# A GRU with a mixture of experts on one core: input product ahead of the steps, preparation in another order

## What is computed

```python
gi = x @ W_ih + b_ih            # 512 -> 3 * 512
gh = h @ W_hh + b_hh
r = sigmoid(i_r + h_r); z = sigmoid(i_z + h_z)
n = tanh(i_n + r * h_n)
h = (1 - z) * n + z * h
```

## Time and profile before

| | us |
|---|---|
| median of 3 runs | 913.2 (912.21 to 913.89) |
| the profiled execution | 913.26 |
| its span in the trace | 911.5 |
| TensorE matmul busy | 810.2 (89%) |
| VectorE busy | 634.6 (70%) |
| ScalarE (ACT) busy | 414.3 (45%) |
| GpSimd (POOL) busy | 178.2 (20%) |

### The profile page before, as it was taken

One profiled execution on the slowest core, in us unless ns is written; L12 is line 12 of the kernel. 1 busy time (PEld: TensorE's weight loads), 2 busy tenths in 40 slices (PEclk: granted clock), 3 DMA queues, 4 the chain that ended last, 5 costly groups with the idle time before them and its releaser, 6 DMA issues.

```text
span 911.5 us, 28124 instructions
## 1 busy us (share of the span) xinstructions
PE 810.2 (89%) x11698; PEld 533.4 (59%) x11699; DVE 634.6 (70%) x2087; ACT 414.3 (45%) x852; POOL 178.2 (20%) x454
## 2 busy tenths in 40 slices
PE   5979899997999999999957145999999999999996
PEld 2436565576999899999947143444444444444442
DVE  6868989765888888888875666766775766774500
ACT  0747566543454454545434302834283347416600
POOL 1002212122333333433320001012102100110011
PEclk9989999998999999999987557999999999999999
DMA  9800000000000000000013561247143715360011
GB/s 343 304 0 2 2 1 3 2 3 3 4 5 4 4 4 5 4 4 4 4 29 160 147 223 47 97 136 208 24 138 94 212 16 186 69 193 12 1 24 23
DMA packets 20165, 62.57 MB, mean 69 GB/s; under 512 B 2064, under 2 KB 2064, under 8 KB 17424
## 3 DMA queue, kind: packets, MB, share of 16 engines
q1 hardware_dynamic: 15744, 52.46, 16.6%
q0 software_dynamic: 3584, 8.42, 5.2%
q10 hardware_dynamic: 720, 0.03, 0.1%
HBM read 52.49 MB, written 12.62 MB: 71 GB/s over the span
## 4 chain that ended last, share of the span: by engine, by line
PE 69%; DVE 20%; issue 4%; ACT 3%; DMA 1%; POOL 0%; DVEq 0%; ACTq 0%; POOLq 0%
PE ps L376 18%; PE ps L538 18%; PE ps L551 18%; PE ps L368 8%; DVE wa L1047 4%; DVE wa L1052 3%; DVE halves L1063 3%; ACT wa L648 2%; PE ps L480 2%; PE ps L386 2%; DVE ocand L1056 1%; PE ps L518 1%; PE ps L526 1%; DMA bg_sb<-in_bg 1%; DVE big L965 1%
## 5 line engine op out<-in xcount | busy, mean ns | idle before, releaser
L376 PE MATMUL ps<-halves,wa 128*128 128x64 f16 x8448 | 290.6, 194 | 7.9 <-DVE halves L1063 1.6
L376 PEld LDWEIGHTS ps<-halves,wa 128*128 128x128 f16 x8448 | 274.2, 98 | 35.4 <-DVE halves L1063 15.9
L538 PE MATMUL ps<-wb,big 128*128 128x512 f16 x768 | 166.9, 379 | 1.5 <-DVE wb L1351 1.5
L551 PE MATMUL ps<-big 128*128 128x512 f16 x768 | 166.9, 379 | 0.0
L648 ACT ACTIVATE wa<-ps,un_gates 128x128 f32<-128x128 f32 x288 | 100.1, 365 | 139.0 <-PE ps L376 132.5
L1047 DVE SCALAR_TENSOR_TENSOR wa<-ps,bhn_s,wa 128x64 f32<-128x64 f32 x288 | 80.2, 278 | 72.2 <-ACT wa L648 72.2
L538 PEld LDWEIGHTS ps<-wb,big 128*128 128x128 f16 x768 | 74.7, 98 | 91.5 <-issue 1.7
L551 PEld LDWEIGHTS ps<-big 128*128 128x128 f16 x768 | 75.2, 98 | 89.9
L653 ACT ACTIVATE wa<-wa,un_gates 128x64 f32<-128x64 f32 x288 | 99.1, 344 | 57.5 <-DVE wa L1052 51.1
L368 PE MATMUL ps<-hx,wb 128*128 128x512 f16 x432 | 109.7, 386 | 4.9 <-DVEq L1022 4.9
L713 ACT ACTIVATE hx<-ps,un_hid_in 128x512 f32<-128x512 f32 x64 | 43.7, 683 | 112.4 <-PE ps L538 112.4
(11 more groups left out here) (178 smaller groups left out, 686.2 us busy)
## 6 DMA issues: line engine op xcount, KB each, us to landing
wa<-in_w SPq DMA_DIRECT2D x32, 1024.0 KB, 5.9
hs_rows<-big SPq DMA_DIRECT2D x8, 516.0 KB, 6.2
big<-in_w_ih SPq DMA_DIRECT2D x3, 1024.0 KB, 11.4
hx<-in_x_t SPq DMA_DIRECT2D x3, 1024.0 KB, 20.2
big<-in_w_hh SPq DMA_DIRECT2D x4, 768.0 KB, 16.5
wa<-in_x_t SPq DMA_DIRECT2D x1, 1024.0 KB, 5.2
hx<-hs_rows,idx POOLq DMA_INDIRECT x16, 3.7
out<-hx,idx_out POOLq DMA_INDIRECT x16, 4.8
```

The source lines that it names most:

```text
L376: mm = pe.matmul(gate_ps[:, j, g, :], whh_parts[:, k, w, (4 * g + j) * P:(4 * g + j + 1) * P], halves[:, src, k, h, :], start=False, stop= ...
L538: mm = pe.matmul(ps[:, m % 2, :], w1p[:, w, k, m * P:(m + 1) * P], tokT[:, t, k, :], start=(k == 0 and n == 0), stop=(k == KD - 1 and n == 2))
L551: mm = pe.matmul(ps[:, 2 + g % 2, :], hid[:, h, k, g * P:(g + 1) * P], w2p[:, w, k, :], start=(k == 0 and n == 0), stop=(k == KH - 1 and n ...
```

## The change

The first loads become eight pieces of 256 KB (128 x 512 float32), x_first and W_ih's first third by k. TensorE's first four tiles go k by k, each when its pieces are there. The 12 tiles of the first chunk use all eight banks (`gi_bank`), and the rough steps wait for all twelve to be kept. `PREFILL` = 24 fills (two tiles) run ahead of the wait for the diagonal; `filled(i)` says how many are done when step i begins, up to 432, so that step 22 has 12 left and step 23 none. `kept_by` and `split_by` follow from it. On VectorE the bias sum comes behind the first maxima, the maxima of W_hh run in a row, and W_ih's low halves, x's and most of the first chunk's r/z low halves move behind gates_known; the maximum of the last two x chunks comes ahead of most of them. POOL fills turn in place of VectorE. ACT rounds W_ih and x ahead of its fourth tile.

```diff
+        PREFILL = 24
+        def filled(i):
+            return min(PREFILL + FILL_STEP * i, 3 * GI_MMS)
+        def gi_bank(t):
+            return t % 8 if t < 12 else 4 + t % 4
+        def kept_by(i):
+            return 12 + (PREFILL if i < 0 else min(filled(i) + FILLS[0], 3 * GI_MMS)) // (3 * KD)
         def split_by(i):
-            return 12 + 3 * (i + (i % STEPS_C == STEPS_C - 1)) // 2
+            return kept_by(i - 1) if i >= 0 else 12
...
-            sp.dma_start(x_first, x_t[:, CHUNK_ORDER[0], :, :]).then_inc(S["x_loaded"][0], 16)
-            for g in range(3):
+            for k in range(KD):
+                sp.dma_start(x_first[:, k, :], x_t[:, CHUNK_ORDER[0], k, :]).then_inc(S["first_loaded"][k], 16)
+                sp.dma_start(wih_sb[:, k, 0:D], wih_src[:, k, 0:D]).then_inc(S["first_loaded"][k], 16)
+            for g in range(1, 3):
...
-                if t >= 4:
-                    pe.wait_ge(S["gi_kept"], t - 3)
+                if t >= 8:
+                    pe.wait_ge(S["gi_kept"], t - 7 if t < 16 else t - 3)
-            pe.wait_ge(S["x_loaded"][0], 16)
-            for m in range(12):
+            for k in range(KD):
+                pe.wait_ge(S["first_loaded"][k], 32)
+                for m in range(4):
+                    mm = pe.matmul(ps[:, gi_bank(m), :], wih_sb[:, k, m * P:(m + 1) * P], x_first[:, k, :],
+                                   start=(k == 0), stop=(k == KD - 1))
...
+            for m in range(4, 12):
...
             def gates_rough(src, i):
-                n = FILL_STEP * i
+                n = filled(i)
...
+            fill(0, PREFILL)
             pe.wait_ge(S["diag_ready"], 1)
             pe.wait_ge(S["whh_high"], KD)
+            pe.wait_ge(S["gi_kept"], 12)
...
-                    fill(FILL_STEP * i, FILL_STEP * i + FILL_STEP)
+                    fill(filled(i), filled(i + 1))
...
-            for m in range(4):
+            for m in range(3):
                 first_tile(m)
-            wih_high(0)
-            wih_high(1)
-            first_tile(4)
-            wih_high(2)
-            first_tile(5)
-            wih_high(3)
+            for k in range(KD):
+                wih_high(k)
+            act.wait_ge(S["x_loaded"][1], 16)
             for k in range(KD):
                 x_high(0, k)
-            first_tile(6)
+            first_tile(3)
+            first_tile(4)
             act.wait_ge(S["gates_known"], 1)
             whh_high(0)
+            first_tile(5)
+            whh_high(1)
+            first_tile(6)
+            whh_high(2)
             first_tile(7)
-            whh_high(1)
-            whh_high(2)
-            first_tile(8)
             whh_high(3)
-            for m in range(9, 12):
+            for m in range(8, 12):
                 first_tile(m)
...
+            for t in range(12, kept_by(-1)):
+                tile(t)
...
-                for t in range(12 + 3 * i // 2, 12 + 3 * (i + 1) // 2):
+                for t in range(kept_by(i - 1), kept_by(i)):
...
             pool.tensor_tensor(warm[:, :], ones[:, 0:1], ones[:, 0:1], ALU.mult).then_inc(S["warmed"], 1)
+            for k in range(KD):
+                pool.tensor_tensor(turn[:, k, 0:P], ident[:, :], ident[:, :], ALU.mult).then_inc(S["turn_ready"], 1)
...
-            dve.wait_ge(S["x_loaded"][0], 16)
+            for k in range(KD):
+                dve.wait_ge(S["first_loaded"][k], 32)
...
-            for k in range(KD):
-                dve.tensor_copy(turn[:, k, 0:P], ident[:, :])
...
-            for m in range(4):
-                rz_low(m)
...
-                if k < KD - 1:
-                    wih_low(k)
-                if k in (1, 2):
-                    rz_low(3 + k)
...
-            wih_low(KD - 1)
-            rz_low(6)
+            rz_low(0)
...
             dve.sem_inc(S["gates_known"], 1)
-            for k in range(KD):
-                x_low((0, k))
-            rz_low(7)
+            wih_low(0)
+            rz_low(1)
             for n in range(2, NC_):
                 dve.wait_ge(S["x_loaded"][n], 16)
             link(dve.tensor_reduce(peak[:, X1:X1 + 1], hx[:, 2 * KD * GCOLS:KD * N], AX.X, ALU.max,
                                    apply_absolute_value=True))
             dve.sem_inc(S["peak_ready"], 1)
+            wih_low(1)
+            rz_low(2)
+            wih_low(2)
+            rz_low(3)
+            wih_low(3)
+            for k in range(KD):
+                x_low((0, k))
+                if k % 2:
+                    rz_low(4 + k // 2)
...
             dve.sem_inc(S["gi_known"], 1)
+            rz_low(6)
+            rz_low(7)
```

More of the change, by code:

```diff
@@ L211, in gru_moe @@
         S["wih_loaded"] = [sem(f"wih_loaded_{g}") for g in range(3)]
+        S["first_loaded"] = [sem(f"first_loaded_{k}") for k in range(KD)]
         S["whh_loaded"] = [sem(f"whh_loaded_{k}") for k in range(KD)]
@@ L244, in gru_moe @@
         GI_MMS = 12 * KD * 3
-        assert FILL_STEP * STEPS_C == GI_MMS
+        PREFILL = 24
+        assert FILL_STEP * STEPS_C == GI_MMS and PREFILL % (3 * KD) == 0
+        def filled(i):
+            return min(PREFILL + FILL_STEP * i, 3 * GI_MMS)
         CHUNK_ORDER = (3, 0, 1, 2)
@@ L258, in gru_moe @@
             (c, 4 * g + j) for c in CHUNK_ORDER[1:] for j in range(KD) for g in range(3))
+        def gi_bank(t):
+            return t % 8 if t < 12 else 4 + t % 4
         def rz_count(t):
             return sum(m < 8 for _, m in TILES[:t])
+        def kept_by(i):
+            return 12 + (PREFILL if i < 0 else min(filled(i) + FILLS[0], 3 * GI_MMS)) // (3 * KD)
         def split_by(i):
-            return 12 + 3 * (i + (i % STEPS_C == STEPS_C - 1)) // 2
+            return kept_by(i - 1) if i >= 0 else 12
+        assert split_by(STEPS_C - 1) >= 24 and split_by(2 * STEPS_C - 1) >= 36 and split_by(FILLED - 1) == 48
+        assert kept_by(2 * STEPS_C - 1) <= 38
         def x_scale(q):
@@ L339, in bank_free @@
             def bank_free(t):
-                if t >= 4:
-                    pe.wait_ge(S["gi_kept"], t - 3)
-            pe.wait_ge(S["x_loaded"][0], 16)
-            for m in range(12):
+                if t >= 8:
[5 more added lines that the diff above has]
+                                   start=(k == 0), stop=(k == KD - 1))
+                    if k == KD - 1:
+                        mm.then_inc(S["gi_mm"], 1)
+            for m in range(4, 12):
                 bank_free(m)
@@ L350, in _ @@
                 for k in range(KD):
-                    mm = pe.matmul(ps[:, 4 + m % 4, :], wih_sb[:, k, m * P:(m + 1) * P], x_first[:, k, :],
+                    mm = pe.matmul(ps[:, gi_bank(m), :], wih_sb[:, k, m * P:(m + 1) * P], x_first[:, k, :],
                                    start=(k == 0), stop=(k == KD - 1))
@@ L367, in fill @@
                         bank_free(tile)
-                    mm = pe.matmul(ps[:, 4 + tile % 4, :], wih_parts[:, w, k, m * P:(m + 1) * P],
+                    mm = pe.matmul(ps[:, gi_bank(tile), :], wih_parts[:, w, k, m * P:(m + 1) * P],
                                    x_parts[:, q, t, k, :], start=(left == 0), stop=(left == KD * 3 - 1))
@@ L471, in _ @@
             pe.wait_ge(S["gru_over"], 1)
-            pe.wait_ge(S["turn_ready"], 1)
+            pe.wait_ge(S["turn_ready"], KD + 1)
             for n in range(NT):
@@ L600, in keep_tile @@
                         act.wait_ge(S["gi_low"], rz_count(t) - GI_RING + 1)
-                    act.activation(gi_full[:, rz_count(t) % GI_RING, :], ps[:, 4 + t % 4, :], ACT.Identity,
+                    act.activation(gi_full[:, rz_count(t) % GI_RING, :], ps[:, gi_bank(t), :], ACT.Identity,
                                    bias=bias_gi[:, q, m:m + 1], scale=sc).then_inc(S["gi_kept"], 1)
                 else:
-                    act.activation(gi[:, c, m % 4, 2, :], ps[:, 4 + t % 4, :], ACT.Identity, bias=bsum_g[:, m:m + 1],
+                    act.activation(gi[:, c, m % 4, 2, :], ps[:, gi_bank(t), :], ACT.Identity, bias=bsum_g[:, m:m + 1],
                                    scale=g_sc).then_inc(S["gi_kept"], 1)
@@ L891, in _ @@
             dve.wait_ge(S["steps_made"], 1)
[L892 to L896, removed]
             link_n = [0]
@@ L921, in _ @@
             for g in range(3):
-                dve.wait_ge(S["wih_loaded"][g], 16)
+                if g > 0:
+                    dve.wait_ge(S["wih_loaded"][g], 16)
                 dve.tensor_reduce(chunk_peak[:, g:g + 1], wih_sb[:, :, g * D:(g + 1) * D], AX.XY, ALU.max,
@@ L925, in _ @@
             link_n[0] += 4
-            dve.wait_ge(S["consts_pool"], 1)
-            for k in range(KD):
-                dve.tensor_copy(turn[:, k, 0:P], ident[:, :])
+            dve.wait_ge(S["small_loaded"], 16 * 5)
+            dve.tensor_tensor(bsum[:, 0:8], bih[:, 0:8], bhh[:, 0:8], ALU.add)
+            dve.tensor_copy(bsum[:, 8:12], bih[:, 8:12]).then_inc(S["bias_ready"], 1)
+            dve.wait_ge(S["bias_ready"], 1)
```

(5 more changed lines are left out.)

## The result

The changed kernel takes 901.4 us (median of 4 runs, 900.63 to 903.28) beside 913.18 (912.21 to 913.89) for the kernel before: ratio 0.987, 95% interval 0.9852 to 0.9889. It is faster by 11.8 us, where 16.4 were forecast, and 901.4 lies just above the range.

The account below looks back on a forecast made before the run. TensorE was taken to bound the kernel (69% of the span, VectorE 20%); -7.45 by step 0, -2.5, -1.04 and -5.4 at later steps sum to -16.4 against 913.26: forecast 896.9, range 893.7 to 901.2.

Parts of the forecast that it names:

- VectorE's preparation: VectorE's work before step 0: starts at 9.9, x_split complete at 50.4, diagonal at 53.5.
- rival (a): TensorE's clock falls before the prefill or at step 8; each costs 1.5 to 2.2: 898.2 to 900.4; chance 0.2.
- (b): Preparation before step 0 later by up to 2.5 us, through late pieces, POOL's copies or ACT's tiles: 898 to 900; chance 0.15.
- TensorE's part: Float32 input product before step 0: starts at 5.2, ends at 48.9 instead of 55.9.
- the serial reading of 21 us: First loads: about 2.0 us per DMA beside its bytes, paid in a row, would land eight pieces after some 21 us.
- ACT's twelve tiles: ACT's work before step 0: twelve tiles kept at 54.8, with short waits for the ring of three.
- POOL's first ordinary operation: POOL after its reduction, before step 0: falls to about 48 in the new order, costing nothing.
- Steps 8, 16 and 20 to 24: Shorter chunk-start waits and fewer late fills: -2.5 at step 8, -1.04 at 16, -5.4 over steps 22 to 24.
- Slower (e): First loads limited per load, so VectorE waits for the last x chunks: 921 at 3.5 us each; chance 0.03.
- Rival (d): Run-ahead gives nothing at steps 22 and 23, held by VectorE's exact chain and splits: 901.3; chance 0.07.
- Rival (c): Shorter idle before step 24 leaves less half clock: up to 2.7 us less, 894.2; chance 0.1.

Follow-up runs that it names:

- the run-ahead alone: Kernel before plus only the run-ahead of 24 fills (filled, kept_by, split_by), with loads, banks and preparation as before: 905.61 us, ratio 0.9893.
- the maxima by piece: Changed kernel with prefill in operand-arrival order, and VectorE taking maxima of x_first and W_ih's first third piece by piece as they land: 895.12 us, ratio 0.9782.
- the reordered fills: Changed kernel with the 24 prefilled products in operand-arrival order and the diagonal, W_hh and kept-tile waits behind step 0's 13 fills: 897.44 us, ratio 0.981.

## Why the prediction was wrong in size

- **The step that failed**: "VectorE's preparation. It no longer waits for the small loads first, but for the fourth pair of pieces, at 9.6 to 10.3 (two megabytes as before); I take 9.9." The pair landed at 12.09 and VectorE started at 12.21. "Two megabytes as before" took the rate from two loads of 1 MB, x_first's in rows of 8 KB; in pieces the rate between 4 and 8 us was 212 GB/s instead of 376. With two loads or with x_first whole VectorE started at 9.71 and 10.02.
- From there the chain held, link by link: W_hh's maxima ended at 33.3 (forecast 31.0), gates were known at 36.4 (33.5), x was split at 53.08 (50.4), the diagonal stood at 56.35 (53.5). Of that lateness 2.3 is the start; 0.5 more came at POOL's reduction, 0.92 us instead of 0.37.
- **The clock.** The idleness before the run-ahead was 4.86 us where I had 1.5, so rival (a) came on top: 9.67 us instead of 8.15. Together 2.8 (prefill at 53.18, not 50.4) and 1.5 (1.7 against the 8.0 that 0.216 each would give) make the 4.5 us. Rivals (a) and (b) had been priced one by one, at 898.2 to 900.4 and 898 to 900, as if apart; but the late piece causes the idleness and the idleness the half clock. Both at once, 901.4, was no case of its own, and the range ended 0.2 us under it.
- TensorE's part was right, a little better: 4.52 for 5.2, and 48.32 for 48.9. Eight pieces were not paid one by one: the four pairs were complete at 4.5, 8.7, 10.7 and 12.1, so the serial reading of 21 us falls here too. ACT's twelve tiles were kept at 57.43 instead of 54.8 (it waited 2.64 us for the ring), and POOL's first ordinary operation came at 52.25 instead of 48, both without cost.
- **Steps 8, 16 and 20 to 24** came out as worked out: -2.4, -1.07 and -5.47 against -2.5, -1.04 and -5.4. Step 22 has 12 fills, step 23 none and takes 5.09 us, and the half clock at step 24 stays (4.42 us idle). Within the -5.47 two errors cancel: step 23 gave 3.44 instead of 3.1, step 24 0.74 instead of 1.04. The idle before step 8 was 2.31 as forecast, and the clock stayed. Here there was luck: in two experiments it did not stay after 2.12 and 2.32, at a cost of 1.6 us over two steps, so 1.6 of the -2.5 was not certain.
- **Slower (e)** did not come about: the last x chunk landed at 32.4, before VectorE was there. Rival (d) is ruled out by the run-ahead alone (38.46 us from step 19 to 24 instead of 44.87). Rival (c), a shorter half clock at step 24, did not show in the changed kernel but did in four of the experiments, where it took 1.0 us off the step and the whole time did not keep it.

Left open in part: how the pieces' delay divides. The last piece landed at 10.31 with the small loads late, at 9.89 and 10.12 with x_first whole, at 9.62 with both whole. The rates between 4 and 8 us say more: 212 to 238 GB/s in the six traces with eight pieces and early small loads, 269 without the small loads, 357 with them and x_first whole. With x_first whole and the small loads early, all five traces have 357 to 376. So x_first whole restores nearly all of the rate with the small loads in place, while holding these back restores about a third of it (57 of 164 GB/s) and 0.9 to 2.2 us of the landing: the two delay the pieces together. Whether it is x_first's rows or the number of loads isn't shown.

## What to carry to other kernels

When a load is cut into pieces, ask when the last one lands as well as the first, and who needs the last: here one engine gained 5 us at its start and the engine that set the end lost 0.4. Order run-ahead work by the arrival of its operands (5.6 us earlier at step 0 here), and give the consumer that waits for all the pieces the same by-piece treatment (1.4 more, in one trace). Rivals that cause each other are one case with one price, their sum.

## What the runs showed of the hardware

- Eight 256 KB pieces in 2 KB rows beside five small loads: 212 GB/s at a DMA share of 0.86 in 4 to 8 us; without the small loads 269 at 0.93; small loads, four such pieces and x_first whole in 8 KB rows 357 at 1.03; small loads and two 1 MB loads 376 at 1.03. Behind loads of 1 MB and 768 KB, a load of 2 to 8 KB landed 6.9 to 13.0 us after its issue.
- Idleness of TensorE at the start of a step: 2.12, 2.32 and 2.40 us were followed by half clock in three kernels (run-ahead alone, x_first whole, no run-ahead), and each lost 1.6 us over that step and the next. The same lengths were not in others: 2.12 with the maxima by piece, 2.32 with the small loads late and with the reordered fills, 2.40 in the kernel before, 2.31 in the changed one. So length alone doesn't decide in this band; what does stays open. After 4.42 us of idleness ahead of step 24 the clock was always halved, for 3.4 or for 6.8 us.
- POOL's reduction over partitions took 0.92 us beside VectorE's tensor_tensor on two SBUF tiles (both started at 33.87), and 0.37 in the kernel before beside a scalar_tensor_tensor that also reads two (and 0.37 again at 43.33 in the changed kernel beside one). Why these differ wasn't tested.
